# Turning the layout of the slot table's one-hots: row numbers innermost

## The reference

```python
h = patch_tokens(x)                       # 64 images x 37 tokens x 192
h = h + attention(layernorm(h))           # 8 heads, relative positions
h = h + moe(layernorm(h))                 # 8 experts, top 2, capacity

def moe(x):                               # T = 2368 tokens, cap = 740
    topv, topi = top_k(x @ Wg, 2)
    w = softmax(topv)
    order = argsort(-w[:, 0])             # the surest tokens first
    e_ids = topi[order].reshape(T * 2)
    oh = one_hot(e_ids, 8)
    pos = (cumsum(oh, 0) * oh).sum(-1) - 1
    keep = pos < cap
    slot = where(keep, e_ids * cap + pos, 8 * cap)
    buf = zeros(8 * cap + 1, 192).at[slot].set(x[tok_rep])
    h = gelu(buf_e @ W1 + b1)             # per expert, 192 -> 768
    out = h @ W2 + b2                     # per expert, 768 -> 192
    return scatter_add(out[slot] * w * keep)
```

## Time and profile before

| what | us |
|---|---|
| median of 3 runs | 615.82 |
| the runs | 614.15 to 616.25 |
| the profiled execution | 611.56 |
| its span, first to last instruction | 609.7 |
| the routing's last piece, from `dest` (396.24) to the first gather (406.65) | 10.4 |

### The profile page before, as it was taken

One profiled execution on the slowest core, in us unless ns is written; L12 is line 12 of the kernel. 1 busy time (PEld: TensorE's weight loads), 2 busy tenths in 40 slices (PEclk: granted clock), 3 DMA queues, 4 the chain that ended last, 5 costly groups with the idle time before them and its releaser, 6 DMA issues.

```text
span 609.7 us, 12386 instructions
## 1 busy us (share of the span) xinstructions
PE 541.8 (89%) x4264; PEld 501.8 (82%) x4264; DVE 440.9 (72%) x1018; ACT 258.9 (42%) x415; POOL 219.5 (36%) x209
## 2 busy tenths in 40 slices
PE   3999588999999999999999786867999999999983
PEld 2999587998999989989999662445899999999982
DVE  8889955677677677776776857553777777877763
ACT  1222443254243342542443115304685595585560
POOL 0266410201202112012021015028587787777464
PEclk9999796999999999999999677669999999999998
DMA  8798435020211201202112027206276466367151
GB/s 207 175 223 260 123 77 140 15 52 0 51 34 17 51 17 34 51 0 51 34 17 51 2 84 209 83 14 159 54 170 147 106 146 150 91 132 153 19 168 32
DMA packets 62009, 54.97 MB, mean 90 GB/s; under 512 B 29204, under 2 KB 52564, under 8 KB 61182
## 3 DMA queue, kind: packets, MB, share of 16 engines
q1 hardware_dynamic: 52830, 46.04, 29.6%
q0 software_dynamic: 9152, 8.59, 8.4%
HBM read 39.32 MB, written 18.27 MB: 94 GB/s over the span
## 4 chain that ended last, share of the span: by engine, by line
PE 47%; DVE 14%; ACT 13%; issue 10%; SPq 5%; DMA 4%; POOL 3%; DVEq 2%; POOLq 1%; ACTq 0%
PE PS L1043 7%; PE PS L733 6%; PE PS L756 6%; PE PS L712 5%; ACT wide L1088 4%; PE PS L1041 4%; ACT hTh L1231 3%; PE PS L740 2%; PE PS L747 2%; PE PS L749 2%; PE PS L748 2%; DVE hTl L1710 2%; PE PS L1018 2%; ACT b2w L1237 2%; PE PS L720 2%
## 5 line engine op out<-in xcount | busy, mean ns | idle before, releaser
L1761 POOL TENSOR_TENSOR rs<-ve,nhalf 111x1 f32<-111x1 f32 (+2 forms) x40 | 26.1, 653 | 270.0 <-DVE ve L1353 188.1
L1895 POOL DMA_INDIRECT running_sums<-ye,gid x42 | 73.1, 1739 | 35.1 <-DVE ye L1734 25.9
L1043 PE MATMUL PS<-w2hl,hTh 128*128 128x384 f32 (+1 forms) x288 | 82.7, 357 | 0.0
L1041 PE MATMUL PS<-w2hl,hTl 128*128 128x192 f32 (+1 forms) x288 | 73.5, 255 | 4.0 <-DVE hTl L1710 4.0
L1869 POOL DMA_INDIRECT xe<-routed_rows,gid x48 | 53.4, 1112 | 43.7 <-DVE gid L1675 29.5
L1018 PE MATMUL PS<-xeT,w1h 128*128 128x370 f32 x288 | 64.3, 331 | 2.1 <-issue 1.4
L1710 DVE TENSOR_TENSOR hTl<-hf,hTh 128x740 fp32r<-128x740 f32 x48 | 44.6, 929 | 24.7 <-ACT hTh L1231 23.2
L1041 PEld LDWEIGHTS PS<-w2hl,hTl 128*128 128x128 f32 (+1 forms) x288 | 53.7, 186 | 6.3 <-issue 5.6
L712 PE MATMUL PS<-xT,wh 128*128 128x222 f32 x264 | 46.9, 287 | 7.4 <-DVE xT L1367 7.4
L1043 PEld LDWEIGHTS PS<-w2hl,hTh 128*128 128x128 f32 (+1 forms) x288 | 53.0, 184 | 0.5
L1018 PEld LDWEIGHTS PS<-xeT,w1h 128*128 128x128 f32 x288 | 50.4, 188 | 2.8 <-issue 1.8
(11 more groups left out here) (243 smaller groups left out, 1289.8 us busy)
## 6 DMA issues: line engine op xcount, KB each, us to landing
wide<-x SPq DMA_DIRECT2D x24, 288.0 KB, 9.1
w1r<-L_ffn_W SPq DMA_DIRECT2D x16, 384.0 KB, 5.0
rel_scores<-wide SPq DMA_DIRECT2D x66, 73.0 KB
w2r<-L_ffn_W SPq DMA_DIRECT2D x8, 576.0 KB, 4.5
w1r<-L_ffn_W SPq DMA_DIRECT2D x16, 192.0 KB, 4.7
wide<-rel_scores SPq DMA_DIRECT2D x22, 111.0 KB, 2.3
out<-running_sums SPq DMA_DIRECT2D x1, 1776.0 KB, 7.4
h_tokens<-narrow SPq DMA_DIRECT2D x24, 72.0 KB, 2.8
```

The costliest lines, as they stand in the source:

```text
L1041: pe.matmul(PS[0:n, bank, 0:D], hTl[:, c, at], w2hl[:, c, 0, :], start=(c == 0), stop=False, skip_group_check=True)
L1043: last = pe.matmul(PS[0:n, bank, 0:2 * D], hTh[:, c, at], both(w2hl[:, c, :, :]), start=False, stop=(c == HC - 1), skip_group_check=True)
L1895: p_.indirect_dma_start(sums, at, ye[0:r, e % 2, n, :], None, bounds_check=B * T + NT * 128 - 1, oob_is_err=True, compute_op=ALU.add).then ...
```

## The change

Four places. `onehot` and `row_no` are laid out as (`j`, row number), so the row numbers are innermost; the iota that fills `row_no` swaps its two steps; a matmul loads `onehot[:, j, :]`, 128 neighbouring numbers; and the comparison takes each number of `inrow` 128 times in a row, where it took a row of 22 numbers 128 times. `dest` stays as it is.

```diff
-        onehot = piece(G, 2 * NG * 128, FP16).rearrange("p (n j) -> p n j", n=128)
-        row_no = piece(G, 2 * NG * 128, FP16).rearrange("p (n j) -> p n j", n=128)
+        onehot = piece(G, 2 * NG * 128, FP16).rearrange("p (j n) -> p j n", n=128)
+        row_no = piece(G, 2 * NG * 128, FP16).rearrange("p (j n) -> p j n", n=128)
...
             for j in range(2 * NG):
                 pe.wait_ge(s_hot, 2 + j // NG)
-                last = pe.matmul(PS[:, 0, 0:E * NT], onehot[:, :, j], dest[:, :, :, j].rearrange("p e n -> p (e n)"),
+                last = pe.matmul(PS[:, 0, 0:E * NT], onehot[:, j, :], dest[:, :, :, j].rearrange("p e n -> p (e n)"),
...
-                v.tensor_tensor(onehot[:, :, at], row_no[:, :, at],
-                                bc(inrow[:, at].rearrange("p (a j) -> p a j", a=1), [G, 128, NG]), ALU.is_equal
+                v.tensor_tensor(onehot[:, at, :], row_no[:, at, :],
+                                bc(inrow[:, at].rearrange("p (j a) -> p j a", a=1), [G, NG, 128]), ALU.is_equal
                                 ).then_inc(s_hot, 1)
...
-            p_.iota(row_no[:, :, :], [[1, 128], [0, 2 * NG]], base=int(-FAR), channel_multiplier=0,
+            p_.iota(row_no[:, :, :], [[0, 2 * NG], [1, 128]], base=int(-FAR), channel_multiplier=0,
```

## The result

The changed kernel takes 616.34 us (median of 16 runs, 614.02 to 619.28), the kernel before, run beside it, 614.03 us (16 runs, 612.59 to 616.25). The ratio is 1.0035, with a 95% interval of 1.0021 to 1.0049: slower by 2.1 us, between 1.3 and 3.0 (the two medians lie 2.3 apart). The forecast was +1.8 us.

The account below looks back on a forecast made before the run. It took the routing chain up to `gid`, which moves the gather and all that follows, as the bound. +1.88 - 0.05 = +1.8 us on a median of 615.82 gave 617.6 us, with an 8 in 10 range of 615.3 to 619.2.

Parts of the forecast that it names:

- The comparison: DVE's L1663 loses its paired rate through the repeated operand: +1.43 us for each of two instructions.
- The upper end: Of the bounds 1620 to 3050 ns for one L1663, the forecast took 3050, with the pairing lost.
- PE's pace: The 44 matmuls of L971 stay 0.1135 us apart, set by reading `dest` at 88-byte steps.
- one interval in the earlier trace: First two matmuls of L971, at full clock: 0.12 us apart, against 0.113 at half clock.
- three candidates: For L971's 113 ns: loads (0.07 us each), array columns (39 or 20 ns), or loads and columns in turn (109 or 90).
- only the weights count: Rival at L971: strided weight loads set the 113 ns, so 616.1 to 616.6 us; chance 0.22.
- The new wait: PE waits 0.45 us on the second L1663 between the two halves of L971's 44 matmuls.
- The sum: In the routing up to `gid`: +1.88 us for the later matmuls, -0.05 for shorter loads, +1.8 in all.
- the 0.3% line: On the whole kernel's time: about 0.3% (1.85 us) is what a measurement can tell from no change.
- the toss: Whole kernel: 617.6 us, 0.30% more, sits on the edge; slower by over 0.3% had 0.41, within 0.53.
- What was hidden: POOL's iota, done 20 us early, costs 0; all but two of PE's 44 shorter loads are covered, -0.05 us.
- The late clock: Rival: PE's clock returns late and slows the first ten expert matmuls by about 2 us, 619.6; chance 0.07.
- that rival's first half: Up to 419.96 PE waits for gathered rows, so half clock there costs nothing.

Follow-up runs that it names:

- e4: Kernel before, layout untouched, with `inrow` kept in 4-byte numbers, which takes away the comparison's paired rate alone; ratio 1.0030.
- e3: Kernel before with `dest` and its small tables, and one-hots and row numbers, in pairs of choice groups, so the comparison repeats two numbers of `inrow`; ratio 1.0057.
- e6: Kernel before with `dest` and one-hots in pairs of choice groups, and `row_no` holding its 128 numbers once, in pairs; 610.45 us against 613.85, ratio 0.9932.
- e7: Kernel after with its comparison in four instructions of 11 choice groups in place of two of 22, PE waiting for each; ratio 1.0023.
- e1: Kernel before with `dest` and its small tables in pairs of choice groups, a matmul's moving numbers 4 bytes apart in place of 88; ratio 0.9949.
- e2: Kernel after with `dest` in pairs of choice groups, moving numbers 4 bytes apart in place of 88; ratio 0.9990.

## Why the prediction was right, step by step

- *The comparison.* The upper end was the one: 3085 ns measured, 3050 forecast from the slope of L1647 and L1649. The reason given for choosing it was weak: L1647 works on 4-byte numbers, which run at the single rate anyway, so it bounds the price of a lost pairing but can't show that the pairing would be lost. The runs show it: e4 has the same 3085 ns for another reason to lose the pairing, and e3 and e6 the paired 1620 with runs of only two numbers. So it is the neighbour that counts, not the length of the run. This fits the Trainium skill's rule on the innermost step (Vector Engine (DVE) Microarchitecture Reference, 5.1 Performance modes), which no row of before could show.
- *PE's pace.* Forecast unchanged and so measured. The argument that the pace did not follow the clock rested on one interval in the earlier trace rows; e7 bears it out with nine matmuls. The moving operand was left over when three candidates had been struck out, and a fourth was not among them: a fixed floor for a load with its matmul, whatever the layout. e1 and e2 rule that out and show what was claimed, that the moving operand's steps of 88 bytes set the pace. The reading of the Trainium skill's cacheline rule (SBUF — State Buffer, Door 1: The DMA port swizzle) in which only the weights count is refuted by the kernel after itself: its weights are neighbours, and its pace is 0.112.
- *The new wait.* Forecast 0.45 us between the halves of L971; between the end of the first 22 matmuls and the next start there is 0.36 (idle), to which 0.19 of the last matmul's 0.30 adds, 0.55 in all against a running train. The 0.1 us more are the comparison's extra 35 ns and a first half shorter by 0.04 (22 x 0.112 against 2.50); the rest, some 0.02, is within the rounding of the rows. The forecast's 0.45 runs from 403.02 to 403.47 and so holds the step of 0.04 from a comparison's end to PE's start; up to 403.43 alone it would be 0.41.
- *The sum.* +1.95 us within the routing against +1.8 forecast, and 2.1 (1.3 to 3.0) measured. The step that was a little short is the comparison's duration: counted from L1646, the second one ends 2.95 us later than before, against 2.86 forecast. That 2.1 us is 0.35% and so beyond the 0.3% line was the toss that the prediction named; it gave the side that came 0.41, the other 0.53 (its three terms add to 0.54). The interval holds that line, so the measurement doesn't settle the toss either.
- *What was hidden stayed hidden.* A load alone shrank by 0.05 us, and all of them gave 0.04 us (after against e4). The iota shrank to 5.1 us off the path.
- *The late clock* did come: half clock lasted to about 414.5 in the profile after, where it ended by 409.6 before. It cost nothing, as that rival's first half said, since PE waits for gathered rows there, and full clock was back before the first expert matmul at 423.59:

```profile
409.40:414.50 5.10, 4.76 (x12) 1.85 (x14) 2.45 (x3) 0.00 (x0) 3.66 (x3) 0.50 0.13 39
414.70:418.00 3.30, 2.01 (x12) 1.04 (x11) 0.00 (x0) 0.00 (x0) 2.42 (x3) 1.00 0.25 72
```

## What to carry to other kernels

A matmul has two operands that are read: before turning the layout of one, find which of the two sets the pace (free loads every 0.07 us, and a pace that stayed at 0.11 at both clock levels, told it here), for the better layout of the other gave PE nothing (0.112 against 0.1135). When a layout puts an operand's repeated number innermost, look for the paired rate: this 2-byte comparison fell to about half of it (3085 ns against 1620), while repeating a pair of numbers kept it (1621) and still brought the other axis to within 4 bytes. A change of layout also changes the instructions that fill the table, however far off the path they are: look at the run length of each (the iota went from 5.5 to 31.0 us).

## What the runs showed of the hardware that I had not expected

- POOL's iota pays for short runs: 5632 numbers took 5.1 us in runs of 128, 5.5 in runs of 44, and 31.0 in runs of two; 256 numbers in runs of two took 1.5 us, so (31.0 - 1.5) / 5376 = 5.5 ns for a number there, against 5.5 us / 5632 = 1.0 ns in runs of 44.
- DVE's 2-byte writes 88 bytes apart cost 1.33 us for 264 numbers, those in 4-byte steps 0.50 (L1652 before and in e1): more than twice as long for a step alone.
- A matmul's moving operand in 4-byte steps costs nothing that shows at half clock (0.040 us for 48 columns, 39 ns by their number), and in 88-byte steps the pace is 0.113 us at half clock and 0.109 at full.
